# Field products of a recommender tower: eight of a tile's 32 product slots turned round, and their sums taken by matmuls with 32-column weights of ones

## What is computed

```python
e = stack([tbl_f[ids[:, f]] for f in 32 fields], axis=1)     # 2048 rows x 32 fields x 64
p, q = e[:, ROW_IDX], e[:, COL_IDX]                          # the 496 pairs i < j
z = einsum('bne,hne,bnh->bn', p, kernel, q)                  # kernel: 64 x 496 x 64
h = concatenate([z, dense_ctx], axis=1)                      # 496 + 16 = 512 columns
h = maximum(h @ W_top1 + b_top1, 0)                          # 512 -> 512
h = maximum(h @ W_top2 + b_top2, 0)                          # 512 -> 256
y = h @ W_top3                                               # 256 -> 1
```

## Time and profile before

| | |
|---|---|
| Median of 3 runs | 914.67 us (913.3 to 919.67) |
| Profiled execution, its own time | 916.32 us |
| Its span, first to last instruction | 914.5 us |
| PE busy | 824.4 us, 90% |
| ACT busy | 811.7 us, 89% |
| DVE busy | 790.7 us, 86% |
| POOL busy | 488.1 us, 53% |
| Mean granted PE clock | 0.989 of full |

### The profile page before, as it was taken

One profiled execution on the slowest core, in us unless ns is written; L12 is line 12 of the kernel. 1 busy time (PEld: TensorE's weight loads), 2 busy tenths in 40 slices (PEclk: granted clock), 3 DMA queues, 4 the chain that ended last, 5 costly groups with the idle time before them and its releaser, 6 DMA issues.

```text
span 914.5 us, 17660 instructions
## 1 busy us (share of the span) xinstructions
PE 824.4 (90%) x4484; PEld 501.1 (55%) x4484; DVE 790.7 (86%) x1024; ACT 811.7 (89%) x6304; POOL 488.1 (53%) x526
## 2 busy tenths in 40 slices
PE   2779899998999989999898999989999898999998
PEld 1336355564655636465564755646555564655657
DVE  1899999789989899889989899978999789988793
ACT  0899999889998999989999899988999889998895
POOL 7777765455555555555555556555555455553000
PEclk9899999999999999999999999989999999999999
DMA  4741111011111111111111111100111011110000
GB/s 117 245 147 28 27 26 21 18 21 21 22 21 19 21 20 23 19 20 22 22 20 21 21 20 21 21 20 17 21 22 20 18 22 20 22 22 15 1 2 1
DMA packets 26983, 28.04 MB, mean 31 GB/s; under 512 B 13561, under 2 KB 14594, under 8 KB 26882
## 3 DMA queue, kind: packets, MB, share of 16 engines
q0 software_dynamic: 16384, 16.81, 9.6%
q1 hardware_dynamic: 10498, 10.11, 3.5%
HBM read 26.87 MB, written 0.01 MB: 29 GB/s over the span
## 4 chain that ended last, share of the span: by engine, by line
PE 54%; ACT 20%; DVE 17%; issue 6%; POOL 2%; DMA 0%; DVEq 0%; POOLq 0%
PE T L462 27%; ACT prod L317 18%; PE psZ L472 18%; DVE prod L376 9%; PE psE L420 6%; DVE z L389 4%; DVE prod_b L376 4%; PE psE L407 2%; POOL E L260 2%; ACT eT L292 1%; PE psE L415 1%; PE T L420 1%; ACT h1T L299 0%; ACT zT L309 0%; DMA E<-tbl,idx 0%
## 5 line engine op out<-in xcount | busy, mean ns | idle before, releaser
L317 ACT ACTIVATE prod<-prod 128x64 f32<-128x64 f32 x3072 | 737.6, 245 | 14.8 <-DVE prod L376 13.0
L260 POOL DMA_INDIRECT E<-tbl,idx x512 | 483.0, 943 | 351.4 <-DVE prod L376 172.8
L317 ACT ACTIVATION_READ_ACCUMULATOR prod<-prod 128x1 f32 x3072 | 585.3, 191 | 0.0
L462 PE MATMUL T<-kst,eT 64*128 64x512 f32 (+5 forms) x2688 | 521.6, 511 | 30.2 <-DVE prod L376 16.8
L376 DVE TENSOR_TENSOR prod<-T,E 128x1024 f32<-128x1024 f32 x288 | 346.6, 1218 | 70.9 <-PE T L462 66.3
L462 PEld LDWEIGHTS T<-kst,eT 64*128 64x128 f32 x2688 | 236.9, 188 | 224.7 <-issue 141.6
L389 DVE TENSOR_REDUCE z<-prod 128x8 f32<-128x512 f32 (+2 forms) x384 | 242.7, 632 | 0.0
L472 PEld LDWEIGHTS psZ<-ident,prod_b 128*128 128x128 f32 x1024 | 155.1, 258 | 34.8 <-issue 33.0
L472 PE MATMUL psZ<-ident,prod_b 128*128 128x128 f32 x1024 | 166.3, 316 | 0.0
L376 DVE TENSOR_TENSOR prod_b<-T,E 128x1024 f32<-128x1024 f32 x96 | 116.6, 1215 | 0.0
L420 PE MATMUL psE<-zT,w 128*128 128x256 f32 (+1 forms) x256 | 65.5, 402 | 27.0 <-ACT eT L292 26.3
(11 more groups left out here) (26 smaller groups left out, 93.3 us busy)
## 6 DMA issues: line engine op xcount, KB each, us to landing
E<-tbl,idx POOLq DMA_INDIRECT x512, 2.4
kst<-K_T SPq DMA_DIRECT2D x28, 256.0 KB, 5.2
w<-W_top SPq DMA_DIRECT2D x1, 1024.0 KB
kst<-K_T SPq DMA_DIRECT2D x4, 192.0 KB, 5.8
w<-W_top SPq DMA_DIRECT2D x1, 512.0 KB
z<-dense_ctx SPq DMA_DIRECT2D x16, 8.0 KB, 1.6
idx<-ids SPq DMA_DIRECT2D x1, 240.0 KB, 6.2
y_out_dram<-y SPq DMA_DIRECT2D x7, 1.0 KB
```

The lines of the kernel that those rows point to most:

```text
L260: nc.gpsimd.indirect_dma_start(out=E[:, u, f, :], out_offset=None, in_=tables[f], in_offset=bass.IndirectOffsetOnAxis(ap=idx[:, t, f:f + 1 ...
L317: last = nc.scalar.activation(x, x, ACT.Copy, accum_out=z[:, t % 2, Z_AT[s] + m:Z_AT[s] + m + 1])
L462: last = nc.tensor.matmul(T[:, s_ring(t, s), x * BANK + m * D:x * BANK + (m + w) * D], eT[rows, i // 2, :], kst[rows, at + m * D:at + (m + ...
```

## The change

- Eight slots of a tile, the cross slots of (group 0, group 2) and (group 0, group 3), are turned. `kst` is now the weight (64 rows by 128 columns, that is two pairs) and `eT` moves (128 columns): eight matmuls for a slot instead of two (L496 of the new kernel). `T` then has pairs and h on the partitions and the batch along the row. DVE multiplies it by `eT` of the right field pair (L390) into `prod_t`, a ring of six slots.
- The sum over h is now a sum over partitions. For each turned slot PE does four matmuls of 256 columns with a 128x32 slice of `ones` as weight, one for each 32 partitions of `psZ` (L520). They come two slots at a time (`sum_burst`), after steps 14, 19, 26 and 32 (step 0 of the next tile). The 64 transposes are gone.
- The 128 sums lie spread over two blocks of 128 rows, padded with rows of zeros in `W_top1`. So the first dense layer has five weight blocks, not four.
- The other 24 slots go to DVE and ACT, always 8 pairs to DVE of 16. The order of slots within a tile is new (`ORDER`), and so are the steps of all uses of `psE`; `eT` has two buffers. For tile 0 the groups' transposes stand after steps -1, 1, 4 and 15; before, after -1, 2, 10 and 20.

```diff
-EVERY = 4
-CHUNKS = {4: range(0, 16), 8: range(16, 32), 12: range(32, 48), 16: range(48, 64)}
+TURNED_RING = 6
+BURST = 2
+SUM_LAG = 3
+QUAD = 32
+ORDER = ("first second",
+         "cross cross first cross second cross",
+         "cross turned cross turned cross first turned cross turned second",
+         "cross cross turned cross cross turned first cross turned cross cross turned second cross")
+TURNED_BLOCKS = {2: (0,), 3: (0,)}
-TR_STEP = (-4, 2, 10, 20)
-Z_STEP = 6
-MLP_STEP = {("l1", 0): (1, 17), ("l1", 1): (1, 21), ("l1", 2): (1, 24), ("l1", 3): (1, 29),
-            ("l2", 0): (2, 16), ("l2", 1): (2, 21), ("l3", 0): (2, 25)}
+TR_STEP = (-4, -1, 4, 15)
+TR_STEP_0 = (-1, 1, 4, 15)
+Z_STEP = 8
+MLP_STEP = {("l1", 0): (1, 11), ("l1", 1): (1, 18), ("l1", 2): (1, 21), ("l1", 3): (1, 25),
+            ("l2", 0): (2, 11), ("l2", 1): (2, 18), ("l3", 0): (2, 22)}
...
-            return {16: 7 if s % 8 == 2 else 8, 12: 5}[SIZE[s]]
+            return {16: 8, 12: 5}[SIZE[s]]
...
+                if kind == "turned":
+                    if s == first_turned[h]:
+                        dve.wait_ge(bank_free, ordinal["tr", t, h] + 1)
+                    n = turned_at[t, s] - TURNED_RING
+                    if n >= 0:
+                        dve.wait_ge(summed, n // BURST + 1)
+                    j = (GF * h) // 2 + a
+                    nc.vector.tensor_tensor(place_turned(t, s).rearrange("p (q b) -> p q b", b=P),
+                                            T[:, s_ring(t, s), :].rearrange("p (q b) -> p q b", b=P),
+                                            eT[:, u, j:j + 1, :].broadcast_to([P, 2 * GS, P]), ALU.mult).then_inc(mult_done, 1)
+                    return
...
+                if kind == "turned":
+                    for m in range(GS):
+                        for x in (0, 1):
+                            rows = slice(x * D, x * D + D)
+                            last = nc.tensor.matmul(T[:, s_ring(t, s), x * BANK + m * P:x * BANK + (m + 1) * P],
+                                                    kst[rows, at + m * P:at + (m + 1) * P], eT[rows, t % 2, GS * g + m, :],
+                                                    start=True, stop=True)
+                    last.then_inc(t_ready, 1)
+                    return
...
-            def sum_chunk(n, hs):
-                if hs.start == 0:
-                    pe.wait_ge(mult_done, batch_end[n] + 1)
-                    if n > 0:
-                        pe.wait_ge(z_block_out, n)
-                for h in hs:
-                    last = nc.tensor.matmul(psZ[:, 0:P], prod_b[:, n % 2, :, h], ident[:, :], is_transpose=True,
-                                            start=(h == 0), stop=(h == D - 1))
-                if hs.stop == D:
-                    last.then_inc(summed, 1)
+            def sum_burst(t, n):
+                pe.wait_ge(mult_done, NS * t + TURNED[BURST * n + BURST - 1] + 1)
+                if n == 0 and t == 0:
+                    pe.wait_ge(ones_1, 2)
+                if n == 0 and t > 0:
+                    pe.wait_ge(z_block_out, t)
+                for k in range(BURST * n, BURST * n + BURST):
+                    p = place_turned(t, TURNED[k])
+                    for c in range(P // QUAD):
+                        last = nc.tensor.matmul(psZ[c * QUAD:(c + 1) * QUAD, 0:2 * P], ones[:, QUAD - 2 - 2 * k:2 * QUAD - 2 - 2 * k],
+                                                p[:, 2 * c * P:(2 * c + 2) * P], start=(k == 0), stop=(k == len(TURNED) - 1))
+                last.then_inc(summed, 1)
```

More of the change, by code:

```diff
@@ L43, in plan @@
     for h in range(fields // GF):
[L44 to L47, removed]
         f = [GF * h + x for x in range(GF)]
[L49 to L53, removed]
+        cross = [(g, a) for g in CROSS_BLOCKS.get(h, ()) for a in range(GS)]
+        turned = [(g, a) for g in TURNED_BLOCKS.get(h, ()) for a in range(GS)]
+        for kind in ORDER[h].split():
+            if kind == "cross":
+                g, a = cross.pop(0)
+                slots.append(((kind, g, h, a), [[(GF * g + 2 * a + x, j) for j in f] for x in (0, 1)]))
+            elif kind == "turned":
+                g, a = turned.pop(0)
+                slots.append(((kind, g, h, a), [[(GF * g + 2 * m + x, j) for m in range(GS) for j in f[2 * a:2 * a + 2]]
+                                                for x in (0, 1)]))
+            elif kind == "first":
+                slots.append(((kind, h, h, None),
+                              [[(f[x], j) for j in f[2:8]] + [(f[4 + x], j) for j in f[6:8]] for x in (0, 1)]))
+            else:
+                slots.append(((kind, h, h, None),
+                              [[(f[2], j) for j in f[4:8]] + [(f[0], f[1]), (f[4], f[5])],
+                               [(f[3], j) for j in f[4:8]] + [(f[3], f[2]), (f[7], f[6])]]))
+        assert not cross and not turned
     return slots
@@ L65, in runs, with z_columns @@
     return out
[L68 to L79, removed]
+def z_columns(slots, dense):
+    at, k, columns = 0, 0, []
+    upright = sum(len(halves[0]) + len(halves[1]) for (kind, *_), halves in slots if kind != "turned")
+    blocks = -(-(upright + dense) // P)
+    for (kind, *_), halves in slots:
+        n = len(halves[0]) + len(halves[1])
+        if kind != "turned":
+            columns.append(list(range(at, at + n)))
+            at += n
+        else:
+            columns.append([blocks * P + q % 2 * P + q // 2 * QUAD + 2 * k + j for q in range(n // 2) for j in (0, 1)])
+            k += 1
+    return columns, upright, (blocks + 2) * P
 def dlrm_tower(nc, dense, ids, tables, W1, b1, W2, b2, W3, KT, out):
@@ L95, in dlrm_tower @@
     K_AT = [sum(SIZE[:s]) for s in range(NS)]
[L96 to L99, removed]
+    UPRIGHT = [s for s in range(NS) if SLOTS[s][0][0] != "turned"]
+    TURNED = [s for s in range(NS) if SLOTS[s][0][0] == "turned"]
+    Z_COLUMNS, DENSE_AT, z_rows = z_columns(SLOTS, DC)
+    Z_AT = {s: Z_COLUMNS[s][0] for s in UPRIGHT}
+    ZB = KC - 2
+    assert z_rows == KC * P and len(TURNED) <= QUAD // 2 and len(TURNED) % BURST == 0
+    assert sum(SIZE) == NP and 2 * D == P and TILES % 2 == 0
     STEPS = TILES * NS
@@ L450, in products @@
                     pe.wait_ge(bank_free, ordinal["tr", t, g] + 1)
-                if kind != "cross":
+                if kind in ("first", "second"):
                     pe.wait_ge(bank_free, ordinal["tr", t, h] + 1)
@@ L523 @@
     pairs = W1.shape[0] - inputs["dense_ctx"].shape[1]
-    columns = z_columns([len(halves[0]) + len(halves[1]) for _, halves in slots], W1.shape[0] - pairs)
-    rows = np.full(W1.shape[0], -1)
+    columns, dense_at, z_rows = z_columns(slots, W1.shape[0] - pairs)
+    W1z = np.zeros((z_rows, W1.shape[1]), W1.dtype)
     for s, (_, halves) in enumerate(slots):
         for m, (i, j) in enumerate(halves[0] + halves[1]):
-            rows[columns[s] + m] = number(i, j)
-    rows[rows < 0] = np.arange(pairs, W1.shape[0])
-    args += [given("W_top1", W1[rows]), given("b_top1", np.asarray(inputs["b_top1"]).reshape(-1, P).T),
+            W1z[columns[s][m]] = W1[number(i, j)]
+    W1z[dense_at:dense_at + W1.shape[0] - pairs] = W1[pairs:]
+    args += [given("W_top1", W1z), given("b_top1", np.asarray(inputs["b_top1"]).reshape(-1, P).T),
              given("W_top2", inputs["W_top2"]), given("b_top2", np.asarray(inputs["b_top2"]).reshape(-1, P).T),
```

98 lines of the change are left out of this document (50 added, 48 removed).

## The result

The changed kernel takes 872.04 us (median of 4 runs, 870.76 to 872.41); the kernel before took 915.56 beside it. The ratio is 0.9517, 95% interval 0.9481 to 0.9554. The prediction was 869 with a range of 847 to 903.

A forecast was written before the change was run, and what follows sets the result against it. DVE's own work bounds each tile (floor 49.4 us), the rest being waits for PE. 914.5 - 50 (tiles 1 to 15: 774 against 824) + 7.2 (start) - 3 (end) = 868.7 of span; forecast 869 us, range 847 to 903.

The forecast's parts named there:

- DVE's floor of 49.7: DVE's own work per tile: 49.4 us now, plus 0.3 because four reductions grow from 7 to 8 pairs.
- Products: PE's matmuls of a turned slot: 0.95 us if the two halves run side by side, 1.9 if not.
- rival 3: Turned slots on PE: halves not side by side, 1.9 us a slot, 891 us in all; chance 0.10 together with rival 4.
- Sums: PE's burst of 16 records replacing transposes: taken as 1.2 us, between 1.05 fully side by side and 3.65 one after another.
- Rival 1: PE's sums: quadrants overlap only by two, 2.35 us a burst, +1.2 a tile, 887 us in all; chance 0.14.
- rival 2: PE's sums: quadrants don't overlap, 3.65 us a burst, about 930 us in all, slower than before; chance 0.14.
- `l1` tiles: Tiles with first dense layer pieces: 49.7 plus DVE stalls of 2.5 at steps 18 to 22 and 0.4 at step 12, 52.6 us.
- the margin of 0.6 us at step 8: ACT leaves a `prod` place 0.6 us before DVE wants it at step 8, so DVE never stalls for ACT.
- Start: Tile 0: PE stands from near 31.5 to 36.3 us for group 2's gather, step 5 begins at 39.6; a loss of 7.2.
- The end: After DVE's last multiplication: no 64 transposes, first dense layer +1.0, 13.7 us behind DVE instead of 16.8; a gain of 3.
- The last tile: The last tile's time, from a step table of its own: 52 us.
- rival 4: PE's clock: more dips to 1.2 GHz, or a DVE multiplication dearer by a tenth, add 10 to 15 us; 0.10 with rival 3.

The follow-up runs named there:

- the serial version: The changed kernel with each sum's weight widened to 128 columns of ones and zeros, so no sums overlap: 1005.8 us, ratio 1.0721 to the kernel before.
- The two runs with a warm end: Changed kernel plus 18 useless matmuls in PE's last pause: 936.11 us, ratio 0.9966; also with tile 0's transposes and third `l1` piece later: 865.31, 0.9466.

## Why the prediction was right, and where it was off

**Right by its mechanism, on kind A.** Tiles 1 to 15 run from 80.75 to 854.22, 773.5 us, and the sum had 774.

- *DVE's floor of 49.7:* tile 1 has no stall and takes 49.07. The 0.3 for larger reductions and the price of a turned multiplication are covered, and the tiles with stalls come to the same 49.1 once these are taken off: the floor was 0.6 too high. It was read from DVE's busy time, 49.4, in tiles with stalls; by the same count the kernel before has 49.1 too.
- *Products:* 0.99 for 0.95. Halves go side by side; rival 3 is out.
- *Sums:* 1.00 for 1.2, even under the lower end of the estimate, 1.05. No row had stood for it, so that column groups overlap fully was a guess that came true. Rival 1 (2.35) and rival 2 (3.65) are out for this kernel; the serial version shows that rival 2 was priced right. The Trainium skill, TensorE: Matmul & The Clock Gate (Part 3: Packing small matmuls), gives 2.38x for three 32-column tiles. The trace has 1.00 for four side by side against 3.65 for the serial form, 3.65x, and record starts 6 to 7 ns apart. The page also has matmuls start and end strictly in program order; starts 6 ns apart don't break that, but the conclusion that I drew for rival 1, a slot of five record times, doesn't follow from it here.
- *Dense layer:* 2.35 for 2.33.
- *`l1` tiles:* 52.05 for 52.6, stalls of 2.94 for 2.9, at steps 12, 19, 20 and 22. *`l2` tiles:* 50.49 for 50.7, with stalls of 1.39 for 1.0; the lower floor makes up for it.
- *ACT:* the margin of 0.6 us at step 8 held: DVE waits for ACT nowhere in these tiles.
- *Start:* tile 1 at 80.75 for 80.8. The pause (5.82 us, to 36.73) and step 5 at 39.87 for 39.6 came as worked out.

**Mis-sized terms.**

- *The end.* It lies 16.4 us behind DVE's last multiplication (854.22 to 870.6), not 13.7. The step "with small things, 13.7" took the dense layer at the upper clock (32 records at 3.82 us plus 8). But behind the pause of 4.20 us the transposes of `z` took 0.89 for some 0.5 and the 40 records 6.28 for 4.78: +1.9; most of the rest is ACT's last sums, done at 856.90, 2.7 behind DVE instead of 2.2. I had used the lower clock behind a pause at the start and didn't ask for it at the end, where the change itself makes the pause by taking away the 9.52 us of transposes. The two runs with a warm end take 2.1 and 3.5 us back.
- *The last tile*, 55.6 for 52: its pieces stand two steps apart, with stalls of 2.25 and 1.75 at steps 18 and 20. One clock dip in tile 13 cost 1.5. Both are balanced by the lower floor, in the `l1` tiles above all, so the sum of 774 is closer than its terms: that is luck.

**What it didn't foresee.** The prediction took the release times of one trace, a few hundredths of a us, as given on every chip. On kind B the increments come up to 4 us late, at bursts and at some slots, and DVE, which has three slots of cover, stands 4.6 us in `l2` and 6.7 in `l1` tiles. The tiles give back 46.4 us, about the whole gain of 50. This isn't rival 2: PE's bursts last 1.0 us there too. Nor is it rival 4, though the granted clock is lower there (0.958 for 0.988 over the run): most of the standing is behind the end of PE's records. Only 0.03 was set aside for something unforeseen that takes back all the gain. That chips of such a kind exist was not to be read from the rows at hand, but it makes the 0.05 for "same" too small.

## What to carry to other kernels

Price the work that is left behind a pause at the lower clock level, and look for pauses that the change itself opens; filling one with idle matmuls paid 2.1 and 3.5 us in the two traces here. A step of a hand-written order is worth what the next engine still has in hand at that place: moving a piece by one or two steps mostly moved the stall (twice), while moving whole chunks apart gave 3% on kind B without removing any work. So before work is made cheaper, run the old work at better steps; here that was done on one kind of chip alone, and the change's gain can't be divided. Before a gain is believed, run both kernels on more than one chip: the same design, with three slots of cover, was 5% better on one and equal on another whose semaphore increments come late.

## What the hardware did that I had not expected

- Four matmuls on four 32-column groups with 128 rows, each reading its own 256 columns, run side by side: 16 records in 1.00 us against 3.65 us, of which 0.14 us is there once a burst.
- On the chips of kind B TensorE's increments came 1.8 to 4.0 us after the end of most bursts (0.04 on kind A) and some 3 us after some slots, as long as gathers were under way, and up to 17 us while 390 GB/s were being loaded. Whether the recording of the trace has a part in it is open. They then came 59 ns apart. VectorE and ScalarE started within 0.03 us of them. The two kernels differ in how much longer they are there: 24.4 us before, 67 us after the change.
- The profile calls such a release "remote", "issue" or by the producer's name, with an idle time that starts long after the producer's last record has ended. The gap between that record and the consumer's start is what shows it.
